# Four chained graph layers on one core: matrix products side by side in quarters of the array, softmax divided after the value products, leaky relu on ScalarE, loops written out

## The reference

```python
# L0: 8 heads of 16; scores over the edges of adj, softmax, values, output projection
scores = einsum('bhid,bhjd->bhij', q, k) / sqrt(16) + adj[:, None] * W_e
attn = softmax(where(adj != 0, scores, -inf), axis=-1)
out = einsum('bhij,bhjd->bhid', attn, v).reshape(b, n, 128) @ W_o.T
# L1: two 1-d convolutions, message passing exp(-dist) * adj, and a GRU cell
# L2: u = adj * exp(e_i + f_j + a_b); out = (u / sum(u)) @ h
# L3: 4 heads of 32, graph attention with a leaky relu of slope 0.2
e = leaky_relu(e_i[..., None] + e_j[..., None, :], 0.2)
attn = softmax(where(adj > 0, e, -9e15), axis=-1)
out = einsum('bhnm,bhmd->bhnd', attn, h)
```

## Time and profile before

| | us |
|---|---|
| median of 3 runs (2151.73 to 2159.11) | 2156.44 |
| span of the profiled execution | 2151.3 |
| PE busy | 1993.5 (93%) |
| DVE busy | 1669.4 (78%) |
| ACT busy | 1344.1 (62%) |
| POOL busy | 733.6 (34%) |

### The profile page before, as it was taken

One profiled execution on the slowest core, in us unless ns is written; L12 is line 12 of the kernel. 1 busy time (PEld: TensorE's weight loads), 2 busy tenths in 40 slices (PEclk: granted clock), 3 DMA queues, 4 the chain that ended last, 5 costly groups with the idle time before them and its releaser, 6 DMA issues. The chain is left out here.

```text
span 2151.3 us, 43160 instructions
## 1 busy us (share of the span) xinstructions
PE 1993.5 (93%) x13642; PEld 1550.2 (72%) x13642; DVE 1669.4 (78%) x4088; ACT 1344.1 (62%) x4769; POOL 733.6 (34%) x925
## 2 busy tenths in 40 slices
PE   5999999999999999999999999999999999999965
PEld 4777877777777777776777877777776777877643
DVE  4577888878878788787888878778787887888764
ACT  3556667666657667566666656666566666667645
POOL 2233343332343233343333343223343333343220
PEclk9999999999999999999999999999999999999986
DMA  2000000000000000000000000000000000000000
GB/s 84 16 21 21 26 26 21 26 21 12 26 27 21 22 11 26 27 26 22 21 11 26 26 27 21 22 11 26 27 26 22 21 11 27 26 26 6 11 6 10
DMA packets 24296, 47.68 MB, mean 22 GB/s; under 512 B 3283, under 2 KB 3284, under 8 KB 23892
## 3 DMA queue, kind: packets, MB, share of 16 engines
q1 hardware_dynamic: 24020, 44.33, 6.4%
HBM read 35.93 MB, written 8.39 MB: 21 GB/s over the span
## 5 line engine op out<-in xcount | busy, mean ns | idle before, releaser
L759 ACT ACTIVATE e<-sc,nm 128x128 f32<-128x128 f32 x1024 | 399.9, 409 | 65.0 <-DVE nm L995 64.9
L766 ACT ACTIVATE pT<-T 128x512 f32<-128x512 f32 x256 | 158.0, 617 | 299.9 <-PE T L462 299.7
L510 PE MATMUL O<-pT,vpad 128*32 128x128 f32 x2048 | 271.6, 276 | 20.7 <-ACT pT L766 20.7
L992 DVE SCALAR_TENSOR_TENSOR sc<-an,rowb,S 128x512 f32<-128x512 f32 x256 | 189.7, 741 | 124.6 <-PE S L490 78.0
L490 PEld LDWEIGHTS S<-kh,qT 128*128 128x128 f32 x2048 | 268.9, 191 | 9.4
L510 PEld LDWEIGHTS O<-pT,vpad 128*32 128x32 f32 x2048 | 202.9, 109 | 99.3 <-issue 47.2
L490 PE MATMUL S<-kh,qT 128*128 128x128 f32 x2048 | 269.9, 275 | 0.0
L421 POOL TENSOR_SCALAR zplus<-tz 128x512 f32<-128x512 f32 x32 | 28.6, 895 | 596.7 <-issue 571.1
L1003 DVE TENSOR_TENSOR p<-e,rec 128x512 f32<-128x512 f32 x256 | 210.4, 822 | 8.8
L759 ACT ACTIVATION_READ_ACCUMULATOR e<-sc,nm 128x1 f32 x1024 | 213.6, 209 | 0.0
L844 ACT ACTIVATE e<-l,nm 128x128 f32<-128x128 f32 x512 | 201.4, 421 | 7.8 <-DVE nm L1139 7.8
(11 more groups left out here) (191 smaller groups left out, 4465.0 us busy)
## 6 DMA issues: line engine op xcount, KB each, us to landing
xt<-in_x_t SPq DMA_DIRECT2D x32, 256.0 KB, 2.7
an<-in_adj_n SPq DMA_DIRECT2D x32, 256.0 KB, 3.1
xn<-in_x_n SPq DMA_DIRECT2D x32, 256.0 KB, 3.7
at<-in_adj_t SPq DMA_DIRECT2D x32, 256.0 KB, 2.7
out_x<-xo SPq DMA_DIRECT2D x32, 256.0 KB, 2.1
wm<-in_mats SPq DMA_DIRECT2D x1, 1472.0 KB, 6.4
wm<-in_mats SPq DMA_DIRECT2D x1, 832.0 KB, 4.5
att<-in_att SPq DMA_DIRECT2D x8, 0.1 KB
```

The source lines that it names most:

```text
L510: last = mm(O[r, b * N:(b + 1) * N], vpad[:, c:c + 32], g(pT0[:, h % 2, :], b), start=(h % 2 == 0 and b == 0), stop=(h % 2 == 1), skip_gro ...
L759: last = fn(g(e0[:, h % 2, :], b), g(sc0[:, h % 2, :], b), ACT.Exp, bias=nm0[:, h % 2, b:b + 1], accum_out=sum0[:, h % 2, b:b + 1])
L766: fn(pT0[:, h % 2, :], T[:, :], ACT.Copy).then_inc(q["pT_ready"], 1)
L992: v.scalar_tensor_tensor(out=sc0[:, h % 2, :], in0=an[p][:, :], scalar=we[:, h:h + 1], in1=S[h % 2][:, :], op0=ALU.mult, op1=ALU.add).then ...
```

## The change

Four things are changed together.

1. **Scores in pairs, in quarters of the array's rows.** The product of a head reads only the 32 rows in which its features lie. `kh` holds two copies of `kT` instead of eight (even and odd heads, zero where the other parity is). Heads are taken in the order 0, 2, 4, 6, 1, 3, 5, 7 (`head`), and two of them, on different row quarters, are issued alternately into `S[0]` and `S[1]`, in slots 0, 2, 4 and 6. A pair starts only when DVE has read both banks.
2. **Value products in quarters of the columns.** The products of four heads, one on each quarter, are issued alternately (`values(t, 0)` in slot 6, `values(t, 1)` in slot 10); those of L3 are all in slot 13.
3. **Softmax is divided on the results.** `e` itself is transposed. For L0 DVE takes the reciprocals of all sums at once (`norm`, slot 8), POOL spreads them to 16 columns for each head (`spread_sums`), PE transposes them (`sums_T`, slot 11), ACT copies that to `recT`, and DVE multiplies it with `O` while it moves it to `oT` (`out_heads`). For L3 DVE multiplies the transposed output with the reciprocals (in `layer3_end`), a pass more before the residual.
4. **Leaky relu on ACT** (`Prelu` in place of `Identity`, same operands and an alpha; the DVE pass is gone), and **no hardware loop**: all 36 steps are written out on every engine. Besides, `em` shares `aT`, and `rr` shares `tr`.

The core of the diff:

```diff
-        kh = sb("kh", [128, H0, W])
+        kh = sb("kh", [128, 2, W])
...
-        p0 = sb("p0", [128, 2, W])
-        pT0 = sb("pT0", [128, 2, W])
+        recx = sb("recx", [128, GB, H0, D0])
+        recT = sb("recT", [128, W])
+        pT0 = sb("pT0", [128, H0, W])
...
-        p3 = sb("p3", [128, 2, W])
-        pT3 = sb("pT3", [128, 2, W])
+        pT3 = sb("pT3", [128, H3, W])
...
+        def head(i):
+
+            return 2 * (i % 4) + i // 4
...
-            for t in range(6):
-                step(t // 2, t % 2, phases_of(t))
-            with eng.Fori(3, GROUPS // 2 - 1) as k:
-                step(k, 0, [True] * 6)
-                step(k, 1, [True] * 6)
-            for t in range(GROUPS - 2, GROUPS + 4):
+            for t in range(GROUPS + 4):
                 step(t // 2, t % 2, phases_of(t))
...
+            pool.tensor_tensor(pair[:, :], headm[:, 0:4], headm[:, 4:8], ALU.add).then_inc(q["parity_set"], 1)
+            pool.wait_ge(q["parity_set"], 1)
+            pool.tensor_tensor(parity[:, :], pair[:, 0:2], pair[:, 2:4], ALU.add).then_inc(q["parity_set"], 1)
...
-            def k_heads_rest(s, heads):
-                for h in heads:
-                    pool.tensor_scalar(kh[:, h, :], kT[:, :], headm[:, h:h + 1], 1.0, ALU.mult, ALU.mult)\
-                        .then_inc(q["kh_ready"], 1)
+                pool.tensor_scalar(kh[:, 1, :], kT[:, :], parity[:, 1:2], 1.0, ALU.mult, ALU.mult)\
+                    .then_inc(q["kh_ready"], 1)
+
+            def spread_sums(s):
+                pool.wait_ge(q["rec_done"], s + 1)
+                wait(pool, q["recT_ps"], s)
+                pool.tensor_copy(recx[:, :, :, :], rec0[:, :, :].unsqueeze(3).broadcast_to([128, GB, H0, D0]))\
+                    .then_inc(q["recx_done"], 1)
...
-            def scores(s, h):
-                if h == 0:
+            def scores(s, i):
+                if i == 0:
...
-                mm(S[h % 2][:, :], identb[:, :], mask0[:, :], start=True, stop=False, skip_group_check=True)
+                pe.wait_ge(q["kh_ready"], 2 * s + i // 4 + 1)
+                wait(pe, q["sc_ready"], 8 * s + i)
+                for j in range(2):
+                    mm(S[j][:, :], identb[:, :], mask0[:, :], start=True, stop=False, skip_group_check=True)
                 for b in range(GB):
-                    last = mm(g(S[h % 2], b), g(qT, b), g(kh[:, h, :], b), start=False, stop=True,
-                              skip_group_check=True)
-                last.then_inc(q["qk_ps"], 1)
+                    for j in range(2):
+                        r = slice(32 * (head(i + j) // 2), 32 * (head(i + j) // 2) + 32)
+                        last = mm(g(S[j], b), qT[r, b * N:(b + 1) * N], kh[r, i // 4, b * N:(b + 1) * N],
+                                  start=False, stop=True, skip_group_check=True)
+                last.then_inc(q["qk_ps"], 2)
...
-                transpose4(T, p0[:, h % 2, :]).then_inc(q["tr_ps"], 1)
...
+                transpose4(T, e0[:, h % 2, :]).then_inc(q["tr_ps"], 1)
+
+            def values(s, e):
+                pe.wait_ge(q["pT_ready"], 8 * s + 4 * e + 4)
...
-                r = slice(32 * (h // 2), 32 * (h // 2) + 32)
                 for b in range(GB):
-                    c = (b * H0 + h) * 32
-                    last = mm(O[r, b * N:(b + 1) * N], vpad[:, c:c + 32], g(pT0[:, h % 2, :], b),
-                              start=(h % 2 == 0 and b == 0), stop=(h % 2 == 1), skip_group_check=True)
+                    for j in range(4):
+                        c = (b * H0 + head(4 * e + j)) * 32
+                        last = mm(O[32 * j:32 * j + 32, b * N:(b + 1) * N], vpad[:, c:c + 32],
+                                  g(pT0[:, 4 * e + j, :], b), start=(e == 0 and b == 0), stop=(e == 1),
+                                  skip_group_check=True)
                 last.then_inc(q["pv_ps"], 1)
+
+            def sums_T(s):
+                pe.wait_ge(q["recx_done"], s + 1)
+                pe.wait_ge(q["pT_ready"], 8 * s + 8)
+                for b in range(GB):
+                    last = nc.tensor.transpose(g(T, b), recx[:, b, :, :].rearrange("p h d -> p (h d)"), ident[:, :])
+                last.then_inc(q["recT_ps"], 1)
...
             def layer3_values(u, i):
-                if 9 <= i < 9 + H3:
-                    h = i - 9
...
+                if i == SLOTS - 1:
+                    pe.wait_ge(q["l3_done"], H3 * u + H3)
+                    pe.wait_ge(q["pT3_ready"], H3 * u + H3)
                     for b in range(GB):
-                        last = mm(L[32 * h:32 * h + 32, 1, b * N:(b + 1) * N], h3[:, b, h * D3:(h + 1) * D3],
-                                  g(pT3[:, h % 2, :], b), start=(b == 0), stop=True, skip_group_check=True)
+                        for h in range(H3):
+                            last = mm(L[32 * h:32 * h + 32, 1, b * N:(b + 1) * N], h3[:, b, h * D3:(h + 1) * D3],
+                                      g(pT3[:, h, :], b), start=(b == 0), stop=True, skip_group_check=True)
...
-                    if l0 and 0 <= i < H0:
+                    if l0 and i < H0 and i % 2 == 0:
                         scores(t, i)
...
-                    if l0 and 0 <= i - 3 < H0 and i not in (7, 8):
-                        values(t, i - 3)
+                    if l0 and i == 6:
+                        values(t, 0)
...
+                    if l0 and i == 10:
+                        values(t, 1)
...
                     if l0 and i == H0 + 3:
+                        sums_T(t)
                         project_out(t)
...
-                        last = fn(g(z3[:, h % 2, :], b), g(L[:, h % 2, :], b), ACT.Identity,
-                                  bias=h3[:, b, N + h:N + h + 1])
-                    last.then_inc(q["z3_ready"], 1)
+                        last = fn(g(l3[:, h % 2, :], b), g(L[:, h % 2, :], b), ACT.Prelu,
+                                  bias=h3[:, b, N + h:N + h + 1], alpha=SLOPE)
+                    last.then_inc(q["l3_done"], 1)
...
                         if i == H0 + 3:
-                            act.wait_ge(q["pv_ps"], 8 * t + 8)
-                            wait(act, q["wo_ps"], t)
-                            fn(oT[:, :], O[:, :], ACT.Copy).then_inc(q["oT_ready"], 1)
+                            act.wait_ge(q["recT_ps"], t + 1)
+                            wait(act, q["oT_ready"], t)
+                            fn(recT[:, :], T[:, :], ACT.Copy).then_inc(q["recT_ready"], 1)
...
-                    if l3 and i == SLOTS - 2:
-                        act.wait_ge(q["pv3_ps"], H3 * (t - 3) + H3)
+                    if l3 and i == SLOTS - 1:
+                        act.wait_ge(q["pv3_ps"], t - 2)
...
-            def norm(s, h):
-                dve.wait_ge(q["exp_done"], 8 * s + h + 1)
-                v.reciprocal(rec0[:, h % 2, :], sum0[:, h % 2, :]).then_inc(q["rec_done"], 1)
-                dve.wait_ge(q["rec_done"], 8 * s + h + 1)
-                wait(dve, q["tr_ps"], 8 * s + h - 1)
-                v.tensor_tensor(per(p0[:, h % 2, :]), per(e0[:, h % 2, :]), wide(rec0[:, h % 2, :]), ALU.mult)\
-                    .then_inc(q["p_ready"], 1)
+            def norm(s):
+                dve.wait_ge(q["exp_done"], 8 * s + 8)
+                wait(dve, q["recx_done"], s)
+                v.reciprocal(rec0[:, :, :], sum0[:, :, :]).then_inc(q["rec_done"], 1)
+
+            def out_heads(s):
+                dve.wait_ge(q["recT_ready"], s + 1)
+                dve.wait_ge(q["pv_ps"], 2 * s + 2)
+                wait(dve, q["wo_ps"], s)
+                v.tensor_tensor(oT[:, :], O[:, :], recT[:, :], ALU.mult).then_inc(q["oT_ready"], 1)
...
+                    if l0 and i == H0:
+                        norm(t)
+                    if l0 and i == H0 + 2:
+                        out_heads(t)
```

More of the change, by code:

```diff
@@ L80, in build @@
         headm = sb("headm", [128, H0])
+        pair = sb("pair", [128, 4])
+        parity = sb("parity", [128, 2])
         sel = sb("sel", [KS, 4])
@@ L140, in build @@
         tz = sb("tz", [128, W])
-        rr = sb("rr", [128, W])
         gn = sb("gn", [128, W])
@@ L167, in build @@
         e3 = sb("e3", [128, 2, W])
-        sum3 = sb("sum3", [128, 2, GB])
-        rec3 = sb("rec3", [128, 2, GB])
-        p3 = sb("p3", [128, 2, W])
-        pT3 = sb("pT3", [128, 2, W])
+        sum3 = [sb(f"sum3{p}", [128, GB, H3]) for p in range(2)]
+        rec3 = sb("rec3", [128, GB, H3])
+        pT3 = sb("pT3", [128, H3, W])
         o3T = sb("o3T", [128, W])
@@ L293, in _ @@
             store(0, 0)
-            with sp.Fori(2, GROUPS // 2 - 1) as k:
+            for k in range(2, GROUPS // 2 - 1):
                 for p in range(2):
@@ L613, in layer2 @@
                     pe.wait_ge(q["x2T_ready"], u + 1)
-                    wait(pe, q["r3_done"], u - 1)
+                    wait(pe, q["n3_done"], u - 1)
                     for b in range(GB):
@@ L764, in probs_T @@
                 act.wait_ge(q["tr_ps"], 8 * s + h + 1)
```

(14 more changed lines are left out.)

113 lines of the change are left out of this document (46 added, 67 removed).

## The result

The changed kernel takes **2108.19 us** (median of 4 runs, 2103.75 to 2109.26), the kernel before 2155.53 us (2151.73 to 2159.11). The ratio is 0.9775, 95% interval 0.9757 to 0.9793: faster by 47 us. The forecast was 1955, with a range of 1830 to 2060. The sign was right, the size was not: 153 us of the expected gain are missing.

What follows compares the result with a forecast made beforehand. The prediction took PE, busy 93%, to bound the kernel. From 2151.3 us it took 50 for the loop, 125 for 29 steps and 25 for the ends, giving 1951; the median lies 5 higher, so 1955, range 1830 to 2060.

Steps and rivals of the forecast that it cites:

- The loop: Steps 6 to 29: writing out the hardware loop gives back 50 us, 4.5 for each return.
- PE's work: Score pairs, value blocks of 32 and transposes of reciprocals: PE's work falls by 10.2 to about 51 us a step.
- The rival with row quarters that don't run side by side: Score pairs: only columns run side by side, a pair costs 2.4, +2.1 us a step, about 2015; chance 0.10.
- ACT keeps its time with Prelu: Leaky relu on ACT: Prelu takes Identity's time, no function switches tables, ACT stays at 42 us a step.
- First part: Step start to transposes of head 3, PE leading: 31.7 us becomes 28.1, with two new waits of PE.
- Second part: Transposes of head 3 to those of head 7, ACT leading: 19.9 us becomes 18.0, -1.9.
- Third part: Transposes of head 7 to the next step's start, a chain over all engines: 10.9 us becomes 12.2, +1.3.
- the sum of the walk: One whole step, its three parts added: 58.3 us against 62.6, -4.3; over steps 3 to 31 -125.
- the -25 at the ends: The seven steps at the program's ends: an estimated 3.5 us less each, -25 in all.
- PE did not stay the bound: Rival for the whole step: PE stays the bound, steps of say 53 us, about 1800; chance 0.18.
- the written-out program is fed fast enough: Rival on the loop: the written-out program is fed too slowly, the 50 us don't come, about 2005; chance 0.05.
- The slower side: Rival for score and value products: nothing runs side by side, 8.8 us more a step, about 2210; chance 0.04.

Runs made afterwards that it cites:

- e1: The kernel before with its hardware loop written out and nothing else changed; 2104.9 us, ratio 0.9763 to the kernel before.
- e4: The changed kernel with the transposes of the reciprocals and ACT's copy of them one slot earlier; 1966.2 us, ratio 0.9116 to the kernel before.
- e9: The kernel before with the loop written out and the scores in pairs, other parts as before; 2121.6 us, ratio 0.9845 to the kernel before.
- e8: The changed kernel with score and value products issued head by head, so neighbours use the same quarter; 2216.7 us, ratio 1.0284 to the kernel before.
- e12: The changed kernel without the late division: loop written out, score pairs, blocks of 32, Prelu on ACT; 1969.6 us, ratio 0.9128 to the kernel before.

## Why the prediction was wrong, step by step

- *The loop: 50 us.* Right (e1: -50.6).
- *PE's work: -10.2 us a step.* The direction was right. A block of 32 instructions was priced at 1.4 us and takes 1.02: four quarters of the columns run side by side where I had rows for two. A pair was priced at 1.5 with its masks and takes 1.61 (1009.20 to 1010.29 and masks of 0.52). The page "TensorE: Matmul & The Clock Gate" of the Trainium skill gives 2.38x for three column tiles, which cannot be set beside four; here four give 4 x 1.00 / 1.02 = 3.9x. The rival with row quarters that don't run side by side fell: two times 0.89 us of products take 1.09 together.
- *ACT keeps its time with Prelu.* Right: 364 ns against 372, and the trace has one load of tables, as before.
- *First part 28.1.* 29.0 at the full clock. The wait for `ll` was sized at 0.8 and is 0.88 to 1.05; the three pairs were 0.11 dearer each, and blocks behind them cost a change of shape.
- *Second part 18.0.* 18.6. ACT starts on the next head 1.6 us behind the mark (1007.67 to 1009.29) where 0.95 was sized, its two waits come to 0.5 us where 1.2 was sized, and the 0.5 that was to be saved at the end did not come.
- *Third part 12.2.* 12.9 at the full clock. The wait for `oT`, with its signals, was right (1.5 predicted; from 1032.0 to 1033.56). The wait for `yT` was sized at 0.6 and is 1.22: I had it queue behind `oT` and the mask, but not beside POOL's `kh`, which starts in the same moment, as `kT` comes late by the same chain. The third transposes of L3 come 3.4 us behind the mark instead of 3.2, and the block of L3 gave 0.4 back.
- **The step that failed** is the sum of the walk, "58.3 us against 62.6", in two terms. The parts were mis-sized by 0.9 + 0.6 + 0.7 = 2.2 us. And the walk took every duration at the full clock, because the two steps of before that I read show 1.00 throughout. In one of them PE was busy for 61.24 of 62.70 us; a chain with four waits within 12 us was new, and that the clock would not outlast it I did not ask. This costs 62.6 - 60.5 = 2.1 us a step. Over 29 steps 64 + 61 = 125 us: just the -125 of the prediction. The rest is the -25 at the ends, none of which came: against e1 the changed kernel reaches its first full step 4.8 us earlier (225.7 against 230.5), but needs 6.5 us more for what follows the last (129.8 against 123.2), at a granted clock of 0.67 where e1 has 0.78.
- *The sign* came true through the loop alone. All the rest of the change was forecast at -150 us and came to +3 against e1.
- *The warning was in the trace of before.* Three of its full steps, each the first behind a return of the loop, have a fall in the first part; in one of them PE waited 1.04 us for the same `ll`, and about 2 us later its clock fell to half for 3.4 us (timeline of PE, then the stretch):

```profile
496.45 1.15 PE L577 MATMUL M<-lr,ll 9*128 9x128 f32 x8 [1.04 <-DVE ll L1026]
```

```profile
498.70:502.20 3.50, 3.50 (x18) 3.37 (x17) 3.04 (x5) 1.12 (x5) 2.25 (x2) 0.51 0.03 5
```

- *The order.* I priced `recx` as covered, which it is (ready 4 us early). But I walked the order as given and did not ask what DVE's wait for `recT` holds up behind it, and so what one slot earlier would be worth. e4 gives the answer: 142 us, nearly all of the 153 that were missing.
- *Rivals.* PE did not stay the bound (83%), the row quarters do run side by side, and the written-out program is fed fast enough (e1). The slower side needed 6.9 us a step from blocks that run one after the other; what came was 4.3 us a step, from waits and clock, with the blocks shorter than forecast. No rival had that mechanism, and so the range ended too low.

## What to carry to other kernels

When work is taken off the leading engine, list the waits that it covered; e9 shows that a step with 2.4 us less work in its score blocks can become 0.5 us *longer*. If a pass waits for a long chain (PE to ACT to DVE), put its input as early as you can, and look at what stands behind it in the engine's order; e4 moved the input by one slot. And where work taken off PE leaves a group of waits of about 1 us each, price the clock on top: some 1.5 us for each fall, mended here by an unread product of 0.85 us in the wait.

## What the runs showed of the hardware

- 32 instructions of 128 columns (16 fp32 products) in four quarters of the columns take 1.02 us when neighbours alternate between the quarters, about the time of 8; 2.39 us when they don't (e8). In two quarters of the rows, 16 instructions take 1.09 us against 1.64.
- The clock fell to its lower level behind waits of PE of only 0.88 to 1.41 us. The Trainium skill, "TensorE: Matmul & The Clock Gate", section "HAM oscillation — how this bites in real kernels", describes falls between bursts of products, with waits for DMA of 3 to 5 us; no wait inside a full step of the changed kernel was near that, and the clock fell all the same. A wait's length alone does not decide: in the changed kernel it fell behind the 0.89 us at 993.57, but not behind the 1.04 us in the same place of the next step. In e12 a wait of 1.40 us stands ahead of the same scores in each step; behind it the clock was 0.53 once and 1.00 the next time (the first and the second row below), and it fell there in 2 of the 28 full steps, in 3 others behind the wait for `ll`. What decides stays open.

```profile
1003.90:1007.30 3.40, 3.40 (x18) 3.35 (x16) 2.79 (x6) 3.17 (x16) 0.00 (x0) 0.53 0.01 5
...
1062.80:1066.50 3.70, 3.69 (x57) 3.11 (x55) 3.09 (x8) 3.58 (x18) 0.00 (x0) 1.00 0.00 0
```

- DVE's `yT` and POOL's `kh` took 1.41 and 1.44 us beside each other, 0.69 and 1.04 in e4, where `kh` starts later. The pass `zn` ahead of `yT` also ran beside `kh` for 0.5 us and kept its 0.68, so what grew was `kh` and then `yT`, each the one that started second.
